# Last 256 tokens of a transformer block's second layer computed with tokens on partitions

## The reference

```python
h = _layernorm(x) * (1 + ca) + sa
x = x + ga * attention(h)            # causal, one head of 128, softmax over 2048 keys
h = _layernorm(x) * (1 + cb) + sb
prob = softmax(h @ w_router + b_router)          # 16 blocks, the best 4 are kept
hid = relu(h @ w1.T + b1)                        # 512 hidden channels in 16 blocks
y = (hid * mask_of_kept_blocks) @ w2.T + b2
x = x + gb * y
```

## Time and profile before

| what | value |
|---|---|
| median of 3 runs | 118.75 us (118.54 to 119.10) |
| span of the profiled execution | 117.1 us |
| PE busy | 110.9 us (95%), 583 instructions |
| DVE, ACT, POOL busy | 86.6, 75.4, 88.7 us |
| TensorE clock granted | full in all of the span but its last 2 us |

### The profile page before, as it was taken

How to read it: one execution, slowest core, us unless ns; L and a number is a source line. 1 busy time by engine, 2 the same in 40 slices (tenths; PEclk the granted TensorE clock), 3 DMA queues, 4 the chain that set the end, 5 groups by cost and what they waited for, 6 DMA issues and landing times.

```text
span 117.1 us, 1992 instructions
## 1 busy us (share of the span) xinstructions
PE 110.9 (95%) x583; PEld 87.7 (75%) x583; DVE 86.6 (74%) x312; ACT 75.4 (64%) x162; POOL 88.7 (76%) x122
## 2 busy tenths in 40 slices
PE   5998799999999999999999999999999999999980
PEld 1477675978888888878867987788889788865770
DVE  5669799998989989999888576825693945874521
ACT  2324968875984099559679959998075577536430
POOL 2566888999797989999896998999966798822000
PEclk9999999999999999999999999999999999999997
DMA  2796000000000000000000000000000000023033
GB/s 57 197 318 194 0 3 3 0 6 0 0 3 0 0 6 0 0 0 3 0 0 0 0 6 0 0 0 0 0 0 6 3 0 3 0 79 100 0 95 90
DMA packets 6290, 3.42 MB, mean 29 GB/s; under 512 B 1157, under 2 KB 5894, under 8 KB 6279
## 3 DMA queue, kind: packets, MB, share of 16 engines
q1 hardware_dynamic: 5846, 3.09, 9.2%
q10 hardware_dynamic: 432, 0.20, 0.6%
HBM read 2.24 MB, written 1.05 MB: 28 GB/s over the span
## 4 chain that ended last, share of the span: by engine, by line
PE 71%; POOL 13%; DVE 6%; ACT 4%; issue 4%; DVEq 0%
PE bank L848 17%; PE bank L852 17%; PE bank L849 16%; POOL p_lo L468 8%; PE bank L894 5%; PE bank L1116 4%; POOL rstd L393 3%; PE bank L965 2%; PE bank L875 2%; ACT xn L540 2%; PE bank L1053 2%; POOL neg_mean L391 1%; PE bank L1026 1%; ACT p_full L571 1%; DVE xn L649 1%
## 5 line engine op out<-in xcount | busy, mean ns | idle before, releaser
L468 POOL TENSOR_TENSOR p_lo<-p_full,p_hi 128x512 fp32r<-128x512 f32 (+2 forms) x36 | 42.4, 1202 | 3.9 <-ACT p_full L571 3.9
L564 ACT ACTIVATE p_hi<-bank 128x512 fp32r<-128x512 f32 (+2 forms) x36 | 20.7, 576 | 9.2 <-PE bank L852 4.6
L571 ACT ACTIVATE p_full<-bank 128x512 f32<-128x512 f32 (+2 forms) x36 | 20.6, 572 | 1.6 <-POOL p_lo L468 1.5
L474 POOL TENSOR_TENSOR hid_lo<-hid_full,hid_hi 128x512 fp32r<-128x512 f32 x12 | 15.8, 1321 | 3.9 <-ACT hid_hi L598 3.9
L675 DVE TENSOR_REDUCE cmax<-bank 128x1 f32<-128x512 f32 x24 | 16.1, 684 | 1.2 <-PE bank L894 1.0
L894 PE MATMUL bank<-zt_hi,g_hi 128*128 128x512 f32 (+3 forms) x40 | 15.6, 403 | 0.4 <-DVE g_hi L698 0.2
L848 PE MATMUL bank<-g_hi,zt_hi 128*128 128x512 f32 (+3 forms) x40 | 14.8, 370 | 0.0
L849 PE MATMUL bank<-g_hi,zt_lo 128*128 128x512 f32 (+3 forms) x40 | 14.6, 365 | 0.0
L852 PE MATMUL bank<-g_lo,zt_hi 128*128 128x512 f32 (+3 forms) x40 | 14.5, 363 | 0.0
L848 PE MATMUL bank<-p_hi,z_hi 128*128 128x512 f32 (+2 forms) x36 | 13.9, 385 | 0.0
L852 PE MATMUL bank<-p_lo,z_hi 128*128 128x512 f32 (+2 forms) x36 | 13.5, 376 | 0.1
(11 more groups left out here) (190 smaller groups left out, 255.9 us busy)
## 6 DMA issues: line engine op xcount, KB each, us to landing
x<-in_L_attn_y_all_dram SPq DMA_DIRECT2D x3, 256.0 KB, 3.9
out_dram<-res SPq DMA_DIRECT2D x3, 256.0 KB, 2.3
w<-in_L_ffn_w_dram SPq DMA_DIRECT2D x2, 256.0 KB, 5.0
x<-in_L_attn_y_all_dram SPq DMA_DIRECT2D x2, 128.0 KB, 2.9
wmod<-in_L_wmod_dram SPq DMA_DIRECT2D x1, 256.0 KB, 4.4
out_dram<-res SPq DMA_DIRECT2D x2, 128.0 KB, 1.8
wmod<-in_L_wmod_dram ACTq DMA_DIRECT2D x1, 128.0 KB, 3.2
wk<-in_L_attn_Wk_dram SPq DMA_DIRECT2D x1, 64.0 KB, 3.0
```

Of the source, the lines that this page charges most:

```text
L468: pool.tensor_tensor(p_lo[:, s, w:], p_full[:, n % 2, w:], p_hi[:, s, w:].bitcast(F32), ALU.subtract).then_inc(p_lo_pool, 1)
L474: pool.tensor_tensor(hid_lo[:, m, :], hid_full[:, n % 2, :], hid_hi[:, m, :].bitcast(F32), ALU.subtract).then_inc(hid_lo_pool, 1)
L564: nc.scalar.activation(p_hi[:, s, w:], src, ACT.Exp).then_inc(p_hi_s, 1)
L571: nc.scalar.activation(p_full[:, n % 2, w:], src, ACT.Exp).then_inc(p_full_s, 1)
```

## The change

1. The last 256 tokens (two tiles of 128) leave the path through `y_sb`. `hid_last` holds their hidden layer whole, in fp32; `down_rows(i)` (steps `t0`, `t1`) makes, for a tile, four fp32 products with the hidden layer as weights and `w2_full` as moving operand, so that the result comes out with tokens on partitions. DVE's `row_finish` adds it to `x_due` and writes `res`. The tiles are stored apart, one by ACT's queue and one by SP's.
2. Gate `gb` is multiplied into w2 before it is transposed (ACT step `z13`, product `z8`). All `y_copy` steps then have no scale any more.
3. The row `gb*b2` is made as a 128x128 product (`z11`) of `gbb2_wide`, copied by ACT (`z14`), and added by POOL (`z12`) to x of the last two tiles, beforehand, giving `x_due`.
4. ACT's Relu of the last group becomes two of 256 columns, DVE's low half one of 256.
5. All four tables are written anew.

```diff
@@ plans (four tables, a piece of one)
-d8 d9 y1 h11 m3 h12 h13 v12 v13 d10 d11 h14 v14 h15 v15 d12 y2 d13 d14 d15 d16 d17 d18 d19 y3 y4
+h12 m3 d9 d10 v12 h13 v13 d11 h14 v14 h15 v15 d12 d13 y2 d14 d15 t0 y3 t1
...
@@ stores
+        def store_row(queue, i):
+            t = GT // 2 + i
+            queue.wait_ge(row_res_s, i + 1)
+            queue.dma_start(out_tiles[NG - 1][:, t:t + 1, :],
+                            res[:, (NG - 1) % 2, t * P:(t + 1) * P].rearrange("p (i d) -> p i d", d=D)).then_inc(stored[NG - 1], 16)
...
-            for n in range(NG + 1):
-                g, part = group_part(n)
+            for n in range(NG):
+                g, part = n, result_part(n)
...
+            store_row(sp, 1)
@@ POOL
-                pool.tensor_scalar(gbb2[:], gate[:, GB:GB + 1], cols[:, B2:B2 + 1], None, ALU.mult).then_inc(gate_s, 1)
+                step(pool.tensor_scalar(gbb2[:], gate[:, GB:GB + 1], cols[:, B2:B2 + 1], None, ALU.mult))
+                pool.tensor_scalar(gbb2_wide[:], ident[:], 0.0, gbb2[:], ALU.mult, ALU.add).then_inc(gate_s, 1)
...
+                elif i == 12:
+                    pool.wait_ge(gbb2_row_s, 1)
+                    pool.wait_ge(turn_out, turn_of[f"o{NG - 1}"] + 2)
+                    for i in range(2):
+                        last = pool.tensor_tensor(x_due[:, i, :], x[:, NT - 2 + i, :], gbb2_row[:], ALU.add)
+                    last.then_inc(x_due_s, 1)
@@ ACT
+                elif i == 13:
+                    act.wait_ge(w2_in_s, 16)
+                    act.wait_ge(gate_s, 1)
+                    nc.scalar.activation(w2_gated[:], w2[:], ACT.Identity, scale=gate[:, GB:GB + 1]).then_inc(w2_gated_s, 1)
+                elif i == 14:
+                    act.wait_ge(gbb2_mm, 1)
+                    nc.scalar.copy(gbb2_row[:], proj_bank[:, 0:P]).then_inc(gbb2_row_s, 1)
+                elif i == 15:
+                    store_row(act, 0)
...
-                    nc.scalar.activation(hid_hi[:, n % NH, :], turned_bank(f"h{n}")[:], ACT.Relu).then_inc(hid_hi_s, 1)
+                    half = GW // 2
+                    nc.scalar.activation(hid_hi[:, n % NH, 0:half], turned_bank(f"h{n}")[:, 0:half], ACT.Relu).then_inc(hid_hi_s, 1)
+                    nc.scalar.activation(hid_last[:, n % NH, :], turned_bank(f"h{n}")[:, half:], ACT.Relu).then_inc(hid_last_s, 1)
@@ DVE
+            def row_finish(i):
+                t = GT // 2 + i
+                if i == 0:
+                    dve.wait_ge(x_due_s, 1)
+                    dve.wait_ge(stored[NG - 3], 16)
+                dve.wait_ge(row_mm, i + 1)
+                nc.vector.tensor_tensor(res[:, (NG - 1) % 2, t * P:(t + 1) * P], row_bank(i)[:, 0:P], x_due[:, i, :],
+                                        ALU.add).then_inc(row_res_s, 1)
@@ PE
+            def down_rows(i):
+                t = i * P
+                for m in range(NH):
+                    pe.wait_ge(hid_last_s, m + 1)
+                    last = mm(row_bank(i)[:, 0:P], hid_last[:, m, t:t + P], tile(w2_full, m), start=(m == 0), stop=(m == NH - 1))
+                last.then_inc(row_mm, 1)
...
-                    pe.wait_ge(w2_in_s, 16)
+                    pe.wait_ge(w2_gated_s, 1)
...
+                elif i == 11:
+                    pe.wait_ge(gate_s, 2)
+                    pe.wait_ge(q_lo_s, NG)
+                    mm(proj_bank[:, 0:P], gbb2_wide[:], ident[:], start=True, stop=True).then_inc(gbb2_mm, 1)
```

More of the change, by code:

```diff
@@ L47 @@
[L47 to L48 removed]
+z0 i4 i3 i7 i9 i6 i2 z1 i11 i0 i8 i1 i10 i5 z2 n0 z6 z3 q0 z4 n1 a0 a1 z9 a2 z5 a3 q1 z8 b0 a4 z7 a5 n2 a6 s0 a7
+s1 a8 q2 a9 s2 a10 s3 a11 w0 a12 w1 b1 w2 w3 a13 n3 a14 s4 a15 a16 s5 s6 a17 a18 s7 s8 a19 a20 s9 w4 a21 s10 a22
+w5 s11 a23 w6 o0 w7 q3 b2 w8 w9 w10 a24 s12 a25 s13 a26 s14 a27 s15 a28 a29 w11 s16 a30 s17 o1 n4 w12 w13 a31
@@ L49 @@
+s18 a32 s19 s20 a33 s21 a34 w14 a35 s22 a36 w15 a37 s23 w16 a38 z11 a39 w17 w18 w19 b3 r0 w20 w21 w22 s24 s25 h0
+s26 m0 h1 w23 n5 s27 s28 o2 r1 w24 w25 s29 w26 s30 s31 w27 w28 d0 m1 w29 s32 n6 h2 s33 s34 s35 r2 s36 s37 h3 s38
+w30 w31 w32 w33 s39 m2 w34 w35 w36 w37 w38 w39 h4 h5 d1 o3 d2 d3 h6 h7 y0 d4 h8 h9 d5 d6 n7 d7 h10 r3 y1 h11 d8
+h12 m3 d9 d10 v12 h13 v13 d11 h14 v14 h15 v15 d12 d13 y2 d14 d15 t0 y3 t1
 """
 SCALAR_PLAN = """
-z0 z1 n0 z3 z6 a1 q0 n1 z8 z4 q1 z5 a2 z9 z12 n2 e0 e1 q2 a3 e2 e3 e4 n3 e5 c0 e6 e7 e8 e9 q3 e10 e11 e12 e13
@@ L52 @@
-c1 e14 e15 e16 e17 e18 a4 e19 e20 e21 z7 n4 e22 e23 a5 e24 c2 e25 e26 m0 e27 e28 n5 e29 e30 h0 e31 a6 e32 e33
-h1 m1 e34 e35 n6 h2 e36 e37 e38 e39 h3 c3 h4 h5 m2 y0 h6 h7 a7 h8 n7 h9 y1 h10 m3 h11 h12 h13 y2 h14 h15 y3 y4
+z0 z1 z3 n0 a1 q0 z4 n1 z13 z12 z5 z6 q1 a2 z8 n2 e0 e1 z9 e2 q2 e3 a3 c0 n3 e4 e5 e6 e7 e8 e9 e10 q3 e11 e12
+e13 e14 c1 a4 e15 e16 e17 n4 e18 e19 e20 z7 a5 e21 e22 e23 e24 e25 m0 e26 c2 n5 e27 z14 h0 h1 e28 e29 e30 a6 m1
+e31 e32 n6 e33 e34 e35 h2 e36 e37 h3 e38 e39 c3 h4 h5 y0 h6 h7 m2 a7 h8 n7 h9 y1 h10 m3 h11 h12 h13 y2 h14 h15
@@ L54 @@
+y3 z15
 """
 VECTOR_PLAN = """
[L56 to L59, removed]
+g0 z1 g1 a0 g2 z3 n0 z10 z11 g3 s0 s1 q0 n1 s2 s3 z5 b0 s4 q1 s5 s6 n2 s7 s8 s9 s10 s11 s12 b1 s13 s14 s15 s16
@@ L60 @@
+q2 s17 s18 i8 s19 i9 s20 s21 s22 n3 s23 i10 i11 x0 b2 g4 s24 s25 s26 s27 q3 s28 s29 s30 z6 x1 g5 s31 s32 s33 i20
+s34 i21 s35 i22 s36 s37 s38 s39 n4 i23 b3 m0 c0 h0 h1 n5 x2 g6 m1 c1 h2 n6 i36 m2 i37 i38 c2 h3 i39 h4 h5 x3 g7
+h6 h7 h8 f0 h9 n7 h10 m3 c3 h11 k12 k13 k14 f1 k15 f2 f3 t0 t1
 """
 GPSIMD_PLAN = """
-z0 z5 p0 z1 z7 p1 u0 z6 p2 z8 u1 p3 l0 l1 z4 l2 u2 l4 l5 l6 l7 l8 l9 l10 z11 u3 z10 l12 l13 l14 l15 l16 p4 l17
-l18 l19 p5 l20 l21 l22 z9 l24 l25 l26 l27 l28 l29 p6 l30 l31 k0 l32 l33 k1 l34 k2 l35 l36 l37 l38 k3 k4 k5 p7
@@ L64 @@
-k6 k7 k8 k9 k10 k11
+z7 z4 z0 z5 z8 p0 z1 p1 u0 z6 p2 u1 z11 p3 l0 l1 l2 l4 l5 l6 l7 l8 l9 l10 u2 p4 l12 z10 l13 l14 l15 l16 l17 l18
+p5 l19 z9 l20 l21 l22 u3 l24 l25 l26 l27 k0 l28 p6 l29 k1 l30 l31 l32 l33 l34 l35 l36 l37 l38 k2 k3 k4 k5 p7 k6
+k7 k8 z12 k9 k10 k11
 """
@@ L606, in y_copy @@
                     act.wait_ge(y_turned, g - 1)
-                nc.scalar.activation(y_sb[:, g % 2, part], y_bank(n)[:, part], ACT.Identity, bias=gbb2[:],
-                                     scale=gate[:, GB:GB + 1]).then_inc(y_out, 1)
+                nc.scalar.activation(y_sb[:, g % 2, part], y_bank(n)[:, part], ACT.Identity, bias=gbb2[:]).then_inc(y_out, 1)
             run(SCALAR_PLAN, {"z": prepare, "a": apply, "n": norm_high, "q": q_high, "e": exps, "c": ctx_copy,
```

41 lines of the change are left out of this document (21 added, 20 removed).

## The result

The changed kernel takes **120.77 us** (median of 4 runs, 120.59 to 121.17), the kernel before beside it on the same chip 118.78 (118.54 to 119.1): ratio 1.0167, 95% interval 1.013 to 1.0204. It is slower by 2.0 us, and 117.6 had been forecast. The profiled span is 119.1 us, before 117.1; the granted clock is full in both, before but for the last 2 us.

A forecast was written before the change was run, and what follows sets the result against it. PE was taken to set the pace in the middle, with one chain behind its last product. Terms -0.65 - 0.25 + 0.1 + 0.22 - 0.4 - 0.2 = -1.18 us took 118.75 to 117.6 us, range 116.7 to 118.7.

The forecast's parts named there:

- the end: First product of the tail to the last addition: 2.56 us against 3.21, without the final wait for ACT, -0.65 us.
- the last store: The final store shrinks from 128 to 64 KB and lands sooner: -0.25 us, bounds 0 and -0.5.
- last stretch, `v12` and `v13` apart: Just ahead of the tail: two formerly adjacent steps, now parted, cost more: +0.1 us, bounds 0 and +0.3.
- new steps ahead of the end: Middle: `z11` adds one fp32 product on PE, +0.22 us; `z13`, `z14` on ACT and `z12` on POOL lie where there is room.
- new order, opening: Opening: group 1's normalisation comes about 1 us sooner, reordering takes part back: -0.4 us, from -0.92 to +1.3.
- new order, middle: Middle: PE's work is unchanged, `spread` leaves POOL: -0.2 us, at most 0.36 us of idle time to gain.
- rival 4: Middle: one stall, PE reaching a low half of POOL's before it is made; 118.7 us, chance 0.07.
- Rival 3: Opening becomes a wait, group 0's 1.3 us delay landing on PE's path: +0.72 us, 119.5 us, chance 0.08.
- the fillers' rival (5): Opening: the clock rises later, with three fillers gone from ahead of the thin products; 118.5 us, chance 0.05.

The follow-up runs named there:

- tail_only: The changed code with the old tables, into which only the new steps are put, against the kernel before: 119.26 us, ratio 1.0003.
- bias_fill: Changed kernel with the choice comparison over five tiles, the bias addition on GpSimd and seven opening fillers, against the kernel before: 118.91 us, ratio 1.0019.
- tail_fill: `tail_only` with six more filler products in the opening, against the kernel before: 118.41 us, ratio 0.9968.

## Why the prediction was wrong

The range 116.7 to 118.7 missed by 2 us, and slower had 0.08. The sum of the prediction, against the profiled executions of the kernel before, the changed one and `tail_only`:

| term | forecast us | measured us |
|---|---|---|
| the end | -0.65 | -0.71 |
| the last store | -0.25 | -0.20 |
| last stretch, `v12` and `v13` apart | +0.1 | +0.32 |
| new steps ahead of the end (`z11` alone forecast) | +0.22 | +0.70 |
| new order, opening (up to `w0`) | -0.4 | -0.9 |
| new order, middle (`w0` to `r3`) | -0.2 | +2.8 |
| sum | -1.18 | +2.0 |

The two rows of the order compare the changed kernel with `tail_only`, which has the old tables. `w0` starts at 23.63 us with `s3` (0.39 us) already done, against 24.11; the second half of `r3` at 102.74 against 100.84. They are single executions, and the opening scatters by 0.7 us.

- **The end**, right: 3.21 to 2.50 us. An fp32 product of 128 columns took 0.22 us, as in the row of the projection. PE had no idle time ahead of `y3`.
- **The last store**, right: landing 1.6 us where the straight line through the earlier trace rows gave 1.55, and 2.31 to 2.11 us in all. (The 64 KB on ACT's queue took 1.9.) The Trainium skill, DMA: Bandwidth & Descriptors, section Anatomy of one DMA, gave -0.15 for this term, as near as the line's -0.25. Its nearly constant 2.0 us, 2.15 for 64 KB as an estimate by its formula, is for another path of issue and is not what the queue of SP shows.
- **Around the end**, too low: the working had 0.11 and 0.19 for the parted shutting products and took 0.1; the runs have the whole 0.3.
- **The new steps**: those on ACT and GpSimd were put at nothing, "on engines with room", and `gbb2_wide` was not in the sum at all. Its 0.37 us on GpSimd reached PE whole, at `n2`, since ACT stood there waiting for GpSimd's result, 0.86 us in `tail_only`.
- **The opening** (-0.4), right in kind: `n1` came 0.95 us sooner, more than foreseen, and PE then waited 0.74 us for `nmax`. On the changed code the new order is worth more than forecast, but the new steps take 0.6 of it. What I missed is the same hold: the scaling of `lift2` on VectorE, two inputs in SBUF, took 1.37 us from 11.47 and 0.37 before, because GpSimd's split `z_lo`, moved by the new order, ran from 11.41 to 12.70.
- **The middle** (-0.2): **the step that failed.** I wrote that PE's work does not change with the order, so that 0.36 us of idle time was all there was to win or lose but for one late subtraction (rival 4, 0.07). In fact the middle lost 2.8 us against the old order (the excess grew by 2.3 against the kernel before). The held comparisons are 1.1 us of it and the bias addition 0.8: without both, in `bias_fill`, the second half of `r3` starts at 100.80 instead of 102.74, though `s0` starts at the same time (19.64 and 19.59). The cause of the other 0.9 stays open; it lies behind `b3`. Rival 4 had the kind (one stall), not the number nor the engine: PE waited for VectorE twice and for ScalarE once, and behind the two losses that were taken apart VectorE and GpSimd blocked each other.
- Rival 3, the slower one, named the opening and group 0. That did not happen. The fillers' rival (5) did not either: the changed kernel's clock held.

The working had a hole: I took each instruction's duration from the kernel before as its own. The line of `chosen`, with 426 to 911 ns for one shape, said there that the duration depends on what GpSimd is doing; I had not asked for it.

## What to carry to other kernels

Where PE is full, a new order has little to win and much to lose, here 0.36 us against 2.8; weigh it by every line whose duration varies in the trace, not by mean durations. On VectorE look for copies, casts and comparisons from SBUF to SBUF, and for instructions with two inputs in SBUF: beside a 1.3 us instruction of GpSimd's they waited for its end or made it stand here, and whoever waits for either pays. A fifth tile or a gap of the other engine took such an instruction out of this (12 additions with an input in PSUM did not vary, 290 to 292 ns). Price every instruction that a change adds by the chain that it stands in, not by the room on its engine. Parts of a change that pay for themselves should be measured without the tables that came with them.

## What the runs showed of the hardware

- A comparison of 128 x 512 fp32 to bf16 in SBUF: 0.43 to 0.47 us when it starts between two GpSimd instructions, and then the subtraction behind it takes 1.49 instead of 1.29; 0.63 to 1.48 us when it starts during a GpSimd subtraction; with five tiles (640 columns) 0.82 us in all of its 39 recorded instances in 13 kernels, never held.
- The hold goes both ways. VectorE's addition with two inputs in SBUF stretched one GpSimd subtraction from 1.29 to 2.17 us, and a GpSimd instruction of 0.23 us to 0.95; a GpSimd split stretched VectorE's from 0.37 to 1.37.
- The page of the profile gives a mean and hides this; the line's minimum and maximum show it.
- The same kernel (`tail_only`) had a mean granted clock of 1.0, 0.985 or 0.97 in different runs, 118.3, 119.4 and 120.2 us. With six filler products of 256 columns in the idle time of the opening 11 of 12 runs had the full clock (`tail_fill`, another chip), without them 4 of 12.
- A store of 64 KB landed after 1.6 us on SP's queue and 1.9 on ACT's, one of 128 KB after 1.8, one of 256 KB after 2.3.
